# Cross-attention of a decoder layer, reordered by key blocks: maxima turned once per tile and sent as rows by DMA, pair sums on GpSimd, loop unrolled

## The chip, the cores and the metric

One core of a Trainium2 chip. The metric is the device time of one execution in microseconds (us), the median of several runs; lower is better.

## What is computed

A pre-norm decoder layer on x of shape (16, 256, 512), float32: windowed self-attention, cross-attention, a mixture-of-experts part. Each adds its output to x. The change touches only the cross-attention:

```python
def _L0_xattn_ref(q, k, v, gamma):      # q = layernorm(x); k = v = ctx
    qh = q.reshape(B, h, dq, Lq)        # B 16, h 8 heads, dq 32, Lq = Lk = 512
    kh = k.reshape(B, h, dq, Lk)
    vh = v.reshape(B, h, dv, Lk)
    qk = jnp.einsum('bhdq,bhdl->bhql', qh, kh) * scale
    sm = jax.nn.softmax(qk, axis=-1)
    ret = jnp.einsum('bhql,bhdl->bhdq', sm, vh)
    return gamma * ret.reshape(B, Dv, Lq)
```

The 256 rows of the sequence play the part of channels (8 heads of 32), and the 512 model dimensions are the positions that attend to each other.

## The kernel before

The kernel runs four stages one behind the other: `layer_norm_1`, `self_attention`, `cross_attention` and `expert_mix`. In `cross_attention` the work is cut into 32 tiles (`TILES`) of 128 partitions, each with four heads (`XPT`) of 32 rows and 512 columns; the 512 keys of a head are four blocks of 128 (`CB`).

Each tile goes through these steps. SyncE (SP) loads the tile of x and of the context. VectorE normalizes x (`normed`, L1002), ScalarE rounds it to the matmul's type (`q_round`, L946), GpSimd computes the remainders of x and of the context and also rounds the context (`split`, L803 to L807). SP writes both parts of each to DRAM (`write_parts`) and reads them back stacked, three parts of 32 rows per head, so that one matmul over 96 rows gives a product of nearly full precision (`read_stacks`, two halves of two heads, L766 and L767). TensorE computes the scores SC, queries on partitions (`scores`, L833, 16 per tile); VectorE takes the negated maxima over the keys from PSUM (`maxima`, L1008) and splits them into two parts (`max_parts`). Four groups of matmuls against the identity turn the maxima of a head into rows (`max_rows`, L842), which ScalarE copies into rows 96 to 127 of the query stack (`max_row`, L941). TensorE then computes the scores a second time, transposed, with the maxima already subtracted (`transposed_scores`, ST, L851), and ScalarE takes the exponential into `prt` (L969). Two kinds of f32 groups of four heads weigh the values (into OB) and sum the exponentials by a matmul with ones (into SU) (`output`, L864), four of each per tile. The sums are turned (`sums_by_query`, L873), inverted on VectorE (`one_over_sums`, L1022), repeated by ScalarE (`repeat`), turned back (`inverses`, L881); VectorE multiplies (`output`, L1026), adds to x (`residual`, L1030) and takes the statistics of the next norm (L1037 to L1046).

The order on each engine is written out by hand in `item`. Heads are the outer loop of a tile: the scores are two heads ahead of the transposed scores, the maximum's rows one, and the output matmuls belong to the tile before (`OUT_AT`). Scores and transposed scores have two PSUM banks each, so a score matmul waits for the maximum two before it:

```python
pe.wait_ge(s_mx, 16 * n + 4 * h + q - 1)
```

The first two and last two tiles are written out; the 28 between run in a hardware loop of 4 tiles a turn (2 on SP, `all_tiles`).

Of the kernel before, what the change touches and what calls it, by code (L numbers as in the profile page):

```python
# [625 lines left out]
def cross_attention(nc, x1, ctx_in, gamma, sq, sk, mv2, mv3, x2, cst):  # L626

    ident = cst["ident"]
    ctx = ExitStack()
    with ctx:
# [10 lines left out]
        KS = PARTS * XD  # L646
        gam = sb("gam", [P, 1], F32)
        tmp = sb("rs_tmp2", [P, 2, TILES], F32)
        rstd = sb("rstd2", [P, TILES], F32)
        cin = sb("cin", [P, 2, D], F32)  # L650
# [3 lines left out]
        qst = [sb(f"qst{i}", [P, XPT, D], F32R) for i in range(2)]  # L654
        kst = [sb(f"kst{i}", [P, XPT, D], F32R) for i in range(2)]
        vt = sb("vt", [P, 2, CB, P], F32)
        prt = [sb(f"xprt{i}", [P, XPT, CB, D], F32) for i in range(2)]
        nmx = sb("xnmx", [P, 2, CB], F32)
        nmp = sb("xnmp", [P, 2, CB, XD], F32R)
# [3 lines left out]
        osb = sb("xosb", [P, D], F32)  # L663
# [3 lines left out]
        agg = sb("agg3", [P, 2], F32)  # L667
        hold = sb("hold3", [P, 1], F32)
        SC = [pb(f"xsc{i}") for i in range(2)]
        ST = [pb(f"xst{i}") for i in range(2)]  # L670
        MB = pb("xmb")
# [5 lines left out]
        s_xi = [sem(f"x_xi{i}") for i in range(2)]  # L677
        s_ci = [sem(f"x_ci{i}") for i in range(2)]
# [3 lines left out]

        s_st = [[sem(f"x_st{i}{k}") for k in range(2)] for i in range(2)]
        s_ones = sem("x_ones")
        s_vt, s_vte = sem("x_vt"), sem("x_vte")
        s_sc = sem("x_sc")
        s_mx = sem("x_mx")
        s_nm = sem("x_nm")
        s_mr = sem("x_mr")
        s_row = sem("x_row")  # L690
        s_ts = sem("x_ts")
        s_exp = sem("x_exp")
        s_pv = sem("x_pv")
        s_oe = sem("x_oe")
        s_sq = sem("x_sq")
        s_ri = sem("x_ri")
        s_rr = sem("x_rr")
        s_rt = sem("x_rt")
        s_on = sem("x_on")
        s_x2 = sem("x_x2")  # L700
        s_bn, s_mv = sem("x_bn"), sem("x_mv")
# [5 lines left out]
        def col(ap, n):  # L707

            return ap[:, n, :] if isinstance(n, int) else ap[:, bass.ds(n, 1), :].rearrange("p o d -> p (o d)")

        def all_tiles(eng, item, unroll=4):

            item(0, 0, True, True, True)
            item(1, 1, False, True, True)

            with eng.Fori(1, 1 + (TILES - 4) // unroll) as i:
                for k in range(unroll):
                    item(unroll * i + (2 - unroll + k), k % 2, False, True, True)
            item(TILES - 2, 0, False, True, False)
            item(TILES - 1, 1, False, False, False)  # L720

        def ahead(n, h, d, more):

            return (n, h + d, True) if h + d < XPT else (n + 1, h + d - XPT, more)

        def stacks(n, t):

            per = 32 * PARTS
            return per * (n // 2 + 1) if isinstance(n, int) else (per // 2) * (n - t) + per

        def loads(n, t):

            return 16 * (n // 2 + 1) if isinstance(n, int) else 8 * (n - t) + 16

        @block.sync
        def _(sp):
            sp.dma_start(gam[:, :], gamma.rearrange("(a b) -> a b", a=1).broadcast_to([P, 1])).then_inc(s_gam, 16)

            def load(n, t, b=None):
                dst = x2[:, n, :] if isinstance(n, int) else x2[:, bass.ds(n, 1), :].rearrange("p o d -> p (o d)")  # L740
                if isinstance(n, int):
                    src, csrc = x1v[n // 2, t], cv[n]
                else:
                    src = x1v[bass.ds(b, 1), t].rearrange("o p d -> (o p) d")
                    csrc = cv[bass.ds(n, 1)].rearrange("o p d -> (o p) d")
                sp.dma_start(dst, src).then_inc(s_xi[t], 16)
                sp.dma_start(cin[:, t, :], csrc).then_inc(s_ci[t], 16)

            def write_parts(count, t):

                sp.dma_start(sq[t].rearrange("h p d -> p h d"), qp[:, :, :].bitcast(F32)).then_inc(s_qw, 16)
                sp.wait_ge(s_klo, count)
                sp.dma_start(sk[t].rearrange("h p d -> p h d"), kp[:, :, :].bitcast(F32)).then_inc(s_kw, 16)

            def parts_written(n):
                sp.wait_ge(s_qw, 16 * n + 16)
                sp.wait_ge(s_kw, 16 * n + 16)

            def read_stacks(t, k):

                hs = slice(2 * k, 2 * k + 2)
                qv = sq[t].rearrange("h (j r) d -> h r j d", j=XPT)
                kv = sk[t].rearrange("h (j r) d -> h r j d", j=XPT)
                for c in range(PARTS):
                    rows = slice(XD * c, XD * (c + 1))
                    sp.dma_start(qst[t][rows, hs, :].bitcast(F32), qv[c // 2][:, hs]).then_inc(s_st[t][k], 16)  # L766
                    sp.dma_start(kst[t][rows, hs, :].bitcast(F32), kv[c % 2][:, hs]).then_inc(s_st[t][k], 16)  # L767

            for t in range(2):
                load(t, t)  # L770
            for t in range(2):
                sp.wait_ge(s_qlo, t + 1)
                write_parts(t + 1, t)
                parts_written(t)
                for k in range(2):
                    read_stacks(t, k)

            def item(n, t, first, more, more2):
                if more2:
                    b = None if isinstance(n, int) else sp.snap((n - t) // 2 + 1)  # L780
                    sp.wait_ge(s_vt, n + 1)
                    sp.wait_ge(s_klo, n + 1)
                    load(n + 2, t, b)
                    sp.wait_ge(s_qlo, n + 3)

                    for k in range(2):
                        sp.wait_ge(s_st[t][k], stacks(n, t))
                    write_parts(n + 3, t)
                    parts_written(n + 2)
                    for k in range(2):  # L790
                        sp.wait_ge(s_ts, 16 * n + 8 * k + 8)
                        read_stacks(t, k)

            all_tiles(sp, item, 2)

        @block.gpsimd
        def _(pool):
            def split(n, t):
                pool.wait_ge(s_ci[t], loads(n, t))
                pool.wait_ge(s_kw, 16 * n)  # L800
                pool.wait_ge(s_qhi, n + 1)
                pool.wait_ge(s_qw, 16 * n)
                nc.gpsimd.tensor_tensor(qp[:, 1, :], xn[:, :], qp[:, 0, :].bitcast(F32),  # L803
                                        ALU.subtract).then_inc(s_qlo, 1)
                nc.gpsimd.tensor_copy(kp[:, 0, :], cin[:, t, :]).then_inc(s_khi, 1)
                pool.wait_ge(s_khi, n + 1)
                nc.gpsimd.tensor_tensor(kp[:, 1, :], cin[:, t, :], kp[:, 0, :].bitcast(F32),  # L807
                                        ALU.subtract).then_inc(s_klo, 1)

            for k, (dst, value) in enumerate(((kst[0][KS:P, :, :].bitcast(F32), 1.0), (ones[:, :], 1.0),  # L810
                                              (kst[1][KS:P, :, :].bitcast(F32), 1.0),
                                              (nmp[:, :, :, :].bitcast(F32), 0.0))):
                nc.gpsimd.memset(dst, value).then_inc(s_ones, 1)
                pool.wait_ge(s_ones, k + 1)
            for t in range(2):
                split(t, t)

            def item(n, t, first, more, more2):
                if more2:
                    split(n + 2, t)  # L820

            all_tiles(pool, item)

        @block.tensor
        def _(pe):
            def early(n, h, k):

                return isinstance(n, int) and 16 * n + 4 * h + k < 2

            def scores(n, t, h, q):  # L830
                if not early(n, h, q):
                    pe.wait_ge(s_mx, 16 * n + 4 * h + q - 1)
                nc.tensor.matmul(SC[q % 2][:, :], qst[t][0:KS, h, q * P:(q + 1) * P], kst[t][0:KS, h, :],  # L833
                                 start=True, stop=True).then_inc(s_sc, 1)

            def max_rows(n, t, h):

                pe.wait_ge(s_nm, 8 * n + 2 * h + 2)
                if not (isinstance(n, int) and n == 0 and h == 0):
                    pe.wait_ge(s_row, 4 * n + h)  # L840
                for q in range(CB):
                    last = nc.tensor.matmul(MB[KS:P, q * P:(q + 1) * P], nmp[:, h % 2, q, :].bitcast(F32), ident[:, :],  # L842
                                            start=True, stop=True)
                last.then_inc(s_mr, 1)
# [640 lines left out]
```

## Time and profile before

| | us |
|---|---|
| median of 3 runs | 3128.82 (3126.6 to 3129.32) |
| profiled execution, its own time | 3131.23 |
| its span | 3129.5 |
| TensorE matmul busy in the span | 2908.0 (93%) |
| VectorE busy | 1889.7 (60%) |
| ScalarE busy | 1082.9 (35%) |
| GpSimd busy | 607.1 (19%) |

Cross-attention runs from about 2025 to 2830 us of the span. The profile is of one execution. PE is TensorE's matmul, PEld its weight load, DVE VectorE, ACT ScalarE, POOL GpSimd, SP SyncE, which issues DMAs. "Granted clock" is TensorE's clock as a share of 2.4 GHz. In a timeline a row is start, length, engine, line, operation, output<-inputs, count; a bracket is the idle time before it and what ended it. A DVE or POOL row begins when the engine has begun the instruction, whether or not it can proceed.

### The profile page before, as it was taken

The numbers are of one execution on the slowest core, as the hardware profiler recorded it, in microseconds if no ns is written. First come the engines' busy times: TensorE is split into PE (matmuls) and PEld (weight loads), VectorE is DVE, ScalarE is ACT, GpSimd is POOL, SyncE is SP. The second block draws the span as 40 slices with busy tenths as digits, with TensorE's granted clock in tenths as the row PEclk, the third lists the DMA queues.
The fourth block names the chain that finished last, engine by engine and source line by source line (L and its number), as shares of the span: only waits on it lengthen the run. The fifth ranks groups of instructions, "written<-read, shape, count | busy, mean of one in ns | idle before, by whom it ended". The sixth has DMA issues, their size and how long they took to land. (4 is left out here: it accounts for less than half of the span.)

```text
span 3129.5 us, 45670 instructions
## 1 busy us (share of the span) xinstructions
PE 2908.0 (93%) x15230; PEld 2163.0 (69%) x15230; DVE 1889.7 (60%) x3899; ACT 1082.9 (35%) x2575; POOL 607.1 (19%) x530
## 2 busy tenths in 40 slices
PE   3799999999999999999999999799999999997974
PEld 2588888888888888888788888544544445447852
DVE  7465565665665665565566666565656656553488
ACT  2222223222223222223222222255555555553321
POOL 2111112221112221112321111111111111100163
PEclk9999999999999999999999999989999999995597
DMA  8411222231122131132232121164444444420002
GB/s 315 155 61 54 81 82 85 79 107 54 60 103 81 68 121 54 55 108 78 71 106 70 54 83 53 69 173 130 123 122 132 134 134 121 128 68 17 0 0 107
DMA packets 166225, 289.33 MB, mean 92 GB/s; under 512 B 13728, under 2 KB 79264, under 8 KB 164000
## 3 DMA queue, kind: packets, MB, share of 16 engines
q1 hardware_dynamic: 166048, 287.14, 28.5%
q8 instruction: 90, 1.47, 0.2%
q14 instruction: 87, 0.71, 0.1%
HBM read 194.81 MB, written 92.27 MB: 92 GB/s over the span
## 5 line engine op out<-in xcount | busy, mean ns | idle before, releaser
L439 PE MATMUL pj<-xnt,whi 128*128 128x512 f32 x2048 | 706.8, 407 | 16.1 <-DMA xnt<-xt_scratch 16.1
L519 ACT ACTIVATE pr<-sc,nmx 128x128 f32<-128x128 f32 (+1 forms) x512 | 211.1, 417 | 936.4 <-DVE nmx L591 936.4
L1008 DVE TENSOR_REDUCE xnmx<-xsc 128x1 f32<-128x512 f32 x512 | 340.0, 688 | 277.6 <-PE xsc L833 241.9
L439 PEld LDWEIGHTS pj<-xnt,whi 128*128 128x128 f32 x2048 | 387.4, 189 | 109.1 <-DMA xnt<-xt_scratch 16.5
L969 ACT ACTIVATE xprt<-xst 128x512 f32<-128x512 f32 x512 | 298.4, 596 | 308.1 <-PE xst L851 305.5
L439 PE MATMUL pj<-xnt,wlo 128*128 128x512 f32 x1024 | 400.2, 391 | 0.0
L394 POOL TENSOR_TENSOR qt<-rot,swp 128x512 f32<-128x512 f32 x128 | 166.1, 1297 | 1129.3 <-DVE swp L572 1129.3
L436 PE MATMUL pj<-whi,xnt 128*128 128x512 f32 x1024 | 351.7, 405 | 0.0
L570 DVE TENSOR_TENSOR rot<-pj,trig 128x512 f32<-128x512 f32 x256 | 177.0, 691 | 230.2 <-PE pj L439 230.2
L833 PE MATMUL xsc<-kst,qst 96*128 96x512 f32 x512 | 248.7, 487 | 46.9 <-DVE xnmx L1008 24.2
L833 PEld LDWEIGHTS xsc<-kst,qst 96*128 96x128 f32 x512 | 99.5, 195 | 275.3 <-DVE xnmx L1008 158.7
L591 DVE TENSOR_REDUCE nmx<-sc 128x1 f32<-128x128 f32 (+1 forms) x512 | 158.6, 352 | 177.5 <-PE sc L465 173.0
L600 DVE TENSOR_SCALAR pr<-pr,rinv 128x128 f32<-128x128 f32 (+1 forms) x512 | 251.4, 532 | 9.0
L436 PEld LDWEIGHTS pj<-whi,xnt 128*128 128x128 f32 x1024 | 192.4, 188 | 45.9
L394 POOL TENSOR_TENSOR kt<-rot,swp 128x512 f32<-128x512 f32 x128 | 165.3, 1292 | 297.5 <-DVE swp L572 297.5
L439 PEld LDWEIGHTS pj<-xnt,wlo 128*128 128x128 f32 x1024 | 194.8, 190 | 34.9
L452 PE MATMUL pj<-whi,ohi 128*128 128x512 f32 x512 | 212.5, 415 | 1.4 <-DVE olo L605 1.4
L851 PE MATMUL xst<-qst,kst 128*128 128x512 f32 x512 | 212.1, 415 | 1.3 <-ACT qst L941 1.3
L579 DVE TENSOR_TENSOR xio<-pj,xio 128x512 f32<-128x512 f32 x128 | 88.5, 692 | 192.2 <-PE pj L452 192.2
L452 PE MATMUL pj<-whi,olo 128*128 128x512 f32 x512 | 201.6, 394 | 0.0
L436 PE MATMUL pj<-wlo,xnt 128*128 128x512 f32 x512 | 199.1, 389 | 0.0
L452 PE MATMUL pj<-wlo,ohi 128*128 128x512 f32 x512 | 199.1, 389 | 0.0
(159 smaller groups left out, 4885.6 us busy)
## 6 DMA issues: line engine op xcount, KB each, us to landing
xnt<-xt_scratch SPq DMA_DIRECT2D x64, 1024.0 KB, 8.0
x_scratch<-xio SPq DMA_DIRECT2D x64, 512.0 KB, 3.6
xio<-x_scratch SPq DMA_DIRECT2D x48, 512.0 KB, 4.1
qst<-sq_scratch SPq DMA_DIRECT2D x192, 128.0 KB, 3.0
kst<-sk_scratch SPq DMA_DIRECT2D x192, 128.0 KB, 3.2
xt_scratch<-parts SPq DMA_DIRECT2D x16, 1024.0 KB, 4.7
sq_scratch<-qp SPq DMA_DIRECT2D x32, 512.0 KB, 2.8
sk_scratch<-kp SPq DMA_DIRECT2D x32, 512.0 KB, 2.8
```

The lines of the kernel that those rows point to most:

```text
L394: nc.gpsimd.tensor_tensor(qk["QK".index(kind)][h][:, :, :].rearrange("p b n -> p (b n)"), rot[r % 2][:, :], swp[r % 2][:, :], ALU.add).the ...
L436: last = nc.tensor.matmul(bank[:, :], moving[:, i * P:(i + 1) * P], wpart[:, w, :], start=(k == 0), stop=(k == 3 * CB - 1))
L439: last = nc.tensor.matmul(bank[:, :], wpart[:, w, i * HD:(i + 1) * HD], moving, start=(k == 0), stop=(k == 3 * CB - 1))
L452: last = nc.tensor.matmul(PJ[n % 3][:, :], o[:, h, tok], w[:, CH_O + h, :], start=(h == 0 and k == 0), stop=(h == HG - 1 and k == 2))
L519: nc.scalar.activation(pr[:, a % 4, lo:hi], SC[a % 2][:, lo:hi], ACT.Exp, bias=nmx[:, a % 4, t:t + 1], accum_out=rsum[:, a % 4, t:t + 1]). ...
L570: nc.vector.tensor_tensor(ro, bank, table(slice(0, P), q), ALU.mult)
L591: nc.vector.tensor_reduce(nmx[:, a % 4, t:t + 1], SC[a % 2][:, lo:hi], AX.X, ALU.max, negate=True).then_inc(s_nmx, 1)
L600: nc.vector.tensor_scalar(pr[:, a % 4, lo:hi], pr[:, a % 4, lo:hi], rinv[:, a % 4, t:t + 1], None, ALU.mult).then_inc(s_pr, 1)
L833: nc.tensor.matmul(SC[q % 2][:, :], qst[t][0:KS, h, q * P:(q + 1) * P], kst[t][0:KS, h, :], start=True, stop=True).then_inc(s_sc, 1)
L851: nc.tensor.matmul(ST[c % 2][:, :], kst[t][:, h, c * P:(c + 1) * P], qst[t][:, h, :], start=True, stop=True).then_inc(s_ts, 1)
L969: nc.scalar.activation(prt[t][:, h, c, :], ST[c % 2][:, :], ACT.Exp).then_inc(s_exp, 1)
L1008: nc.vector.tensor_reduce(nmx[:, h % 2, q:q + 1], SC[q % 2][:, :], AX.X, ALU.max, negate=True).then_inc(s_mx, 1)
```

## The change

The head loop and the key-block loop of a tile change places. A step s is one key block c of a tile n (s = 4n + c), with the four heads inside. In a step TensorE issues, for i = 0 to 3, a score matmul of step s+6 (`AHEAD`, a head of the tile one and a half ahead) and the transposed score of head i, after i = 1 some other work (`middle`), and last the output group of step s-1. All loops are unrolled in Python.

The 16 columns of maxima of a tile are turned by one transpose into MX, rounded by ScalarE and their remainder taken by VectorE, and two DMAs place them as rows 96 and 97 of the query stack; the key stack has ones there. The exponentials lie in a ring of five buffers, one per step. GpSimd adds those of two steps in place (`pair_sum`, 128x2048), and TensorE's sums with ones run on the pairs, two groups a tile. The context is rounded by ScalarE. Stacks are three deep, loads four, and each stack is read by six DMAs in place of twelve. The memsets that held scheduling apart and the copy of the statistics go.

```diff
         PARTS = 3
         KS = PARTS * XD
+        KM = KS + 2
+        AHEAD = 6
+        RING = 5
+        STACKS = 3
...
@@ sync @@
+            def read_stacks(m):
+                sp.wait_ge(s_qw, 16 * m + 16)
+                sp.wait_ge(s_kw, 16 * m + 16)
+                if m >= STACKS:
+                    sp.wait_ge(s_ts, 16 * (m - STACKS) + 16)
...
+            def max_rows(m):
+                for k, (part, here) in enumerate(((mhi, s_mhi), (mlo, s_mlo))):
+                    sp.wait_ge(here, m + 1)
+                    row = qst[m % STACKS][KS + k:KS + k + 1, :, :].rearrange("o h (q n) -> o (h q) n", n=P)
+                    sp.dma_start(row.bitcast(F32), part[:, :].bitcast(F32)).then_inc(s_row[m % STACKS], 16)
+
+            for n in range(-4, TILES):
+                if tile(n + 2):
+                    read_stacks(n + 2)
+                if tile(n + 1):
+                    max_rows(n + 1)
+                if tile(n + 3):
+                    write_parts(n + 3)
+                if tile(n + 4):
+                    load(n + 4)
@@ gpsimd @@
+            def pair_sum(n, k):
+                s = CB * n + 2 * k
+                a, b = prt[s % RING], prt[(s + 1) % RING]
+                pool.wait_ge(s_exp, 4 * (s + 1) + 4)
+                pool.wait_ge(s_pv, s + 1)
+                nc.gpsimd.tensor_tensor(a[:, :, :].rearrange("p h n -> p (h n)"), a[:, :, :].rearrange("p h n -> p (h n)"),
+                                        b[:, :, :].rearrange("p h n -> p (h n)"), ALU.add).then_inc(s_add, 1)
...
+            for n in range(-3, TILES + 1):
+                if tile(n - 1):
+                    pair_sum(n - 1, 1)
+                if tile(n + 3):
+                    split(n + 3)
+                if tile(n):
+                    pair_sum(n, 0)
@@ tensor @@
+            def scores(g, q):
+                m, h = g // CB, g % CB
+                if h == 0 and q == 0:
+                    pe.wait_ge(s_st[m % STACKS], 16 * 2 * PARTS * (m // STACKS + 1))
+                if 4 * g + q >= 2:
+                    pe.wait_ge(s_mx, 4 * g + q - 1)
...
+            def transposed_scores(s, h):
+                n, c = s // CB, s % CB
+                if c == 0 and h == 0:
+                    pe.wait_ge(s_row[n % STACKS], 32 * (n // STACKS + 1))
+                if 4 * s + h >= 2:
+                    pe.wait_ge(s_exp, 4 * s + h - 1)
...
+            def sums(n, k):
+                pe.wait_ge(s_add, 2 * n + k + 1)
...
+            def max_transposes(n):
+                pe.wait_ge(s_mx, 16 * n + 16)
+                pe.wait_ge(s_mlo, n)
+                nc.tensor.transpose(MX[0:XPT * CB, 0:P], nmx[:, n % 2, :], ident[:, :]).then_inc(s_mt, 1)
...
+            def middle(n, c):
+                if c == 0:
+                    if tile(n - 1):
+                        sums(n - 1, 0)
+                    if tile(n):
+                        values(n)
+                if c == 1 and tile(n - 2):
+                    inverses(n - 2)
+                if c == 2:
+                    if tile(n - 1):
+                        sums(n - 1, 1)
+                    if tile(n + 1):
+                        max_transposes(n + 1)
+                if c == 3 and tile(n - 1):
+                    sums_by_query(n - 1)
+
+            for s in range(FIRST, LAST):
+                for i in range(XPT):
+                    if 0 <= s + AHEAD < STEPS:
+                        scores(s + AHEAD, i)
+                    if 0 <= s < STEPS:
+                        transposed_scores(s, i)
+                    if i == 1:
+                        middle(s // CB, s % CB)
+                if 0 <= s - 1 < STEPS:
+                    weigh(s - 1)
@@ scalar, keys are (key block, head) @@
+            WORK = {(0, 1): ((repeat, -2),), (0, 2): ((v_evac, 0),), (1, 0): ((output_evac, -1),), (1, 1): ((q_round, 3),),
+                    (1, 2): ((k_round, 3),), (2, 2): ((max_round, 1),), (2, 3): ((sums_evac, -1),)}
@@ vector @@
+            def max_rest(n):
+                dve.wait_ge(s_mhi, n + 1)
+                nc.vector.tensor_tensor(mlo[:, :], MX[0:XPT * CB, 0:P], mhi[:, :].bitcast(F32),
+                                        ALU.subtract).then_inc(s_mlo, 1)
...
+            WORK = {(0, 0): ((normed, 3),), (2, 0): ((output, -2),), (2, 1): ((residual, -2),), (2, 2): ((max_rest, 1),),
+                    (3, 0): ((statistics, -2),), (3, 1): ((mean_and_variance, -2),), (3, 3): ((one_over_sums, -1),)}
+
+            for s in range(FIRST, LAST):
+                n, c = s // CB, s % CB
+                for q in range(XPT):
+                    if 0 <= s + AHEAD < STEPS:
+                        maximum(s + AHEAD, q)
+                    for do, d in WORK.get((c, q), ()):
+                        if tile(n + d):
+                            do(n + d)
```

## Rows read from the trace of the kernel before

**Rows 1.** Busy time by windows: us, busy PE PEld DVE ACT POOL (count), PEclk, DMA, GB/s

```profile
2047.60:2790.60 743.00, 718.58 (x4377) 367.28 (x4376) 452.69 (x1007) 434.18 (x769) 93.53 (x90) 0.97 0.46 129
2132.40:2155.10 22.70, 22.70 (x145) 11.62 (x144) 14.75 (x34) 14.10 (x25) 3.12 (x3) 1.00 0.46 132
2177.80:2208.90 31.10, 27.39 (x146) 14.11 (x145) 14.97 (x35) 14.10 (x25) 3.12 (x3) 0.84 0.36 102
...
1524.50:1527.70 3.20, 3.20 (x9) 2.52 (x8) 2.50 (x6) 0.20 (x1) 1.28 (x1) 0.50 0.87 328
```

**Rows 2.** Groups by line, page of the profile: busy us, mean ns, idle before

```profile
L969 ACT ACTIVATE xprt<-xst 128x512 f32<-128x512 f32 x512 | 298.4, 596 | 308.1 <-PE xst L851 305.5
...
L1030 DVE SCALAR_TENSOR_TENSOR x<-xonm,gam,x 128x512 f32 x28 | 21.1, 752 | 0.0
```

**Rows 3.** Timeline of one tile, 2405 to 2412 us: start, us, engine, line

```profile
2405.49 0.50 PE L833 MATMUL xsc<-kst,qst 96*128 96x512 f32 x1
...
2405.83 0.40 PE L851 MATMUL xst<-qst,kst 128*128 128x512 f32 x1
...
2406.03 0.69 DVE L1008 TENSOR_REDUCE xnmx<-xsc 128x1 f32<-128x512 f32 x1
2406.07 0.60 PE L911 MATMUL xvb<-ident,cin 128*128 128x128 f32 x4
...
2406.42 0.48 PE L833 MATMUL xsc<-kst,qst 96*128 96x512 f32 x1
...
2408.63 0.40 PE L833 MATMUL xsc<-kst,qst 96*128 96x512 f32 x1
...
2408.86 0.39 PE L851 MATMUL xst<-qst,kst 128*128 128x512 f32 x1
...
2409.18 1.06 PE L864 MATMUL xob<-xprt,vt 128*32 128x512 f32 x8
...
2410.18 0.50 PE L833 MATMUL xsc<-kst,qst 96*128 96x512 f32 x1
...
2410.74 0.95 PE L873 MATMUL xvb<-ident,xssb 128*128 128x4 f32 x8
...
2411.55 0.48 PE L833 MATMUL xsc<-kst,qst 96*128 96x512 f32 x1
```

**Rows 4.** Timeline of the first layer norm, 24 to 26 us: VectorE beside GpSimd

```profile
24.15 1.27 POOL L155 TENSOR_TENSOR wlo<-wraw,whi 128x512 fp32r<-128x512 f32 x1 [2.53 <-ACT whi L212]
...
24.90 0.81 DVE L166 TENSOR_SCALAR xn<-x_all,mv,rstd 128x512 f32<-128x512 f32 x1
```

**Rows 5.** Timeline of the threshold search, 2979 us on: VectorE beside GpSimd

```profile
2979.61 1.29 POOL L1296 TENSOR_TENSOR z<-z,eb 128x512 f32 x1
...
2979.72 1.22 DVE L1375 TENSOR_TENSOR thr<-thr,add 128x16 int32<-128x16 int32 x1
...
2980.97 0.18 DVE L1377 TENSOR_TENSOR cand<-thr,bits 128x16 int32<-128x16 int32 x1
```

**Rows 6.** Durations of GpSimd lines, ns min/median/max

```profile
L1286 POOL TENSOR_TENSOR held_out<-hold x32: 194/194/647, 2954.2 to 3085.4; 128x1 f32<-128x1 f32 x32
L803 POOL TENSOR_TENSOR qp<-xn,qp x32: 1262/1282/1288, 2026.6 to 2757.0; 128x512 fp32r<-128x512 f32 x32
L805 POOL CAST kp<-cin x32: 604/611/617, 2027.8 to 2758.2; 128x512 fp32r<-128x512 f32 x32
```

**Rows 7.** Timeline of TensorE at 1523 us, idle time in brackets

```profile
1522.99 0.67 PE L484 MATMUL ob<-prt,v 128*128 128x256 f32 x2 [2.21 <-DVE olo L605]
```

**Rows 8.** DMA view, 2400 to 2448 us: GB/s in 40 slices

```profile
GB/s 237 5 253 232 219 253 200 224 328 36 0 0 0 0 0 0 85 352 237 200 36 234 234 220 253 193 210 302 73 0 0 0 0 0 0 14 384 251 225 17
```

**Rows 9.** Timeline at both ends of the cross-attention

```profile
2038.25 1.19 PE L833 MATMUL xsc<-kst,qst 96*128 96x512 f32 x2 [22.54 <-DMA kst<-sk_scratch]
...
2829.87 0.17 DVE L1046 COPY mv<-agg 128x2 f32<-128x2 f32 x1
```

More of the change, by code:

```diff
@@ L662, in cross_attention @@
         rrep = sb("xrrep", [P, CB, P], F32)
-        osb = sb("xosb", [P, D], F32)
+        osb = [sb(f"xosb{i}", [P, D], F32) for i in range(2)]
         ssb = sb("xssb", [P, D], F32)
@@ L676, in cross_attention @@
         s_gam, s_var, s_sqrt, s_step = sem("x_gam"), sem("x_var"), sem("x_sqrt"), sem("x_step")
[L677 to L678 removed]
+        s_xi = [sem(f"x_xi{i}") for i in range(4)]
+        s_ci = [sem(f"x_ci{i}") for i in range(4)]
         s_qn, s_qhi, s_qlo = sem("x_qn"), sem("x_qhi"), sem("x_qlo")
@@ L705, in cross_attention, with tile @@
         x1v = x1.rearrange("b p t d -> b t p d")
[L707 to L733, printed above, removed]
+        FIRST, LAST = -4 * CB, CB * (TILES + 2)
+        def tile(n):
+            return 0 <= n < TILES
         @block.sync
@@ L778, in item @@
[L778 to L792, printed above, removed]
@@ L824, in _ @@
+            for i in range(STACKS):
+                nc.gpsimd.memset(kst[i][KS:KM, :, :].bitcast(F32), 1.0).then_inc(s_ones, 1)
+                pool.wait_ge(s_ones, i + 1)
+            nc.gpsimd.memset(ones[:, :], 1.0).then_inc(s_ones, 1)
+            for n in range(-3, TILES + 1):
[5 more added lines that the diff above has]
+                    pair_sum(n, 0)
         @block.tensor
@@ L825, in _ @@
         def _(pe):
[L826 to L844, printed above, removed]
@@ L846, in transposed_scores @@
-            def transposed_scores(n, t, h, c):
-                if c == 0:
-                    pe.wait_ge(s_row, 4 * n + h + 1)
-                if not early(n, h, c):
-                    pe.wait_ge(s_exp, 16 * n + 4 * h + c - 1)
-                nc.tensor.matmul(ST[c % 2][:, :], kst[t][:, h, c * P:(c + 1) * P], qst[t][:, h, :],
-                                 start=True, stop=True).then_inc(s_ts, 1)
-            def output(n, t, c, banks=(0, 1)):
-                if c == 0 and 0 in banks:
-                    pe.wait_ge(s_exp, 16 * n + 16)
-                    pe.wait_ge(s_vte, n + 1)
-                    pe.wait_ge(s_oe, 2 * n)
-                for k in banks:
-                    for h in range(XPT):
-                        rows = slice(XD * h, XD * (h + 1))
-                        last = nc.tensor.matmul((OB, SU)[k][rows, :], (vt[:, t, c, rows], ones[:, :])[k],
-                                                prt[t][:, h, c, :], start=(c == 0), stop=(c == CB - 1))
-                if c == CB - 1 and 1 in banks:
-                    last.then_inc(s_pv, 1)
+            def scores(g, q):
[4 more added lines that the diff above has]
+                    pe.wait_ge(s_mx, 4 * g + q - 1)
+                nc.tensor.matmul(SC[q % 2][:, :], qst[m % STACKS][0:KS, h, q * P:(q + 1) * P],
+                                 kst[m % STACKS][0:KS, h, :], start=True, stop=True).then_inc(s_sc, 1)
@@ new lines, in transposed_scores, with weigh @@
+            def transposed_scores(s, h):
[4 more added lines that the diff above has]
+                    pe.wait_ge(s_exp, 4 * s + h - 1)
+                nc.tensor.matmul(ST[h % 2][:, :], kst[n % STACKS][0:KM, h, c * P:(c + 1) * P],
+                                 qst[n % STACKS][0:KM, h, :], start=True, stop=True).then_inc(s_ts, 1)
+            def weigh(s):
+                n, c = s // CB, s % CB
+                pe.wait_ge(s_exp, 4 * s + 4)
+                pe.wait_ge(s_vte, n + 1)
+                if c == 0:
+                    pe.wait_ge(s_oe, n)
+                for h in range(XPT):
+                    rows = slice(XD * h, XD * (h + 1))
+                    last = nc.tensor.matmul(OB[rows, :], vt[:, n % 2, c, rows], prt[s % RING][:, h, :],
+                                            start=(c == 0), stop=(c == CB - 1))
+                last.then_inc(s_pv, 1)
@@ new lines, in sums, with values @@
+            def sums(n, k):
+                pe.wait_ge(s_add, 2 * n + k + 1)
+                if k == 0:
+                    pe.wait_ge(s_se, n)
+                for h in range(XPT):
+                    rows = slice(XD * h, XD * (h + 1))
+                    last = nc.tensor.matmul(SU[rows, :], ones[:, :], prt[(CB * n + 2 * k) % RING][:, h, :],
+                                            start=(k == 0), stop=(k == 1))
+                last.then_inc(s_su, 1)
+            def values(n):
+                pe.wait_ge(s_ci[n % 4], 16 * (n // 4 + 1))
+                if n >= 2:
+                    pe.wait_ge(s_ri, n - 1)
+                for c in range(CB):
+                    last = nc.tensor.transpose(VB[:, c * P:(c + 1) * P], cin[:, n % 4, c * P:(c + 1) * P], ident[:, :])
+                last.then_inc(s_vt, 1)
@@ L926, in _ @@
-            all_tiles(pe, item)
-            for c in range(CB):
-                output(TILES - 1, 1, c)
-            for n in (TILES - 2, TILES - 1):
-                pe.wait_ge(s_vte, TILES)
-                pe.wait_ge(s_x2, n + 1)
-                sums_by_query(n)
-                inverses(n)
+            def middle(n, c):
[13 more added lines that the diff above has]
+                    sums_by_query(n - 1)
@@ L995, in _ @@
             dve.wait_ge(s_gam, 16)
-            nc.vector.memset(hold[:, :], 0.0).then_inc(s_x2, 1)
-            def normed(n, t):
-                dve.wait_ge(s_xi[t], loads(n, t))
-                dve.wait_ge(s_qlo, n)
-                i = slice(n, n + 1) if isinstance(n, int) else bass.ds(n, 1)
-                nc.vector.tensor_scalar(xn[:, :], col(x2, n), mv2[:, i, 0], rstd[:, i],
-                                        ALU.subtract, ALU.mult).then_inc(s_qn, 1)
-            def maxima(n, h, banks):
-                for q in banks:
-                    dve.wait_ge(s_sc, 16 * n + 4 * h + q + 1)
-                    nc.vector.tensor_reduce(nmx[:, h % 2, q:q + 1], SC[q % 2][:, :], AX.X, ALU.max,
-                                            negate=True).then_inc(s_mx, 1)
@@ L1011, in max_parts, with normed @@
-            def max_parts(n, h):
-                dve.wait_ge(s_mx, 16 * n + 4 * h + 4)
-                if not (isinstance(n, int) and n == 0 and h < 2):
-                    dve.wait_ge(s_mr, 4 * n + h - 1)
-                nc.vector.tensor_copy(nmp[:, h % 2, :, 0], nmx[:, h % 2, :]).then_inc(s_nm, 1)
-                dve.wait_ge(s_nm, 8 * n + 2 * h + 1)
-                nc.vector.tensor_tensor(nmp[:, h % 2, :, 1], nmx[:, h % 2, :], nmp[:, h % 2, :, 0].bitcast(F32),
-                                        ALU.subtract).then_inc(s_nm, 1)
+            def normed(m):
+                dve.wait_ge(s_xi[m % 4], 16 * (m // 4 + 1))
+                dve.wait_ge(s_qlo, m)
+                nc.vector.tensor_scalar(xn[:, :], x2[:, m, :], mv2[:, m, 0:1], rstd[:, m:m + 1],
+                                        ALU.subtract, ALU.mult).then_inc(s_qn, 1)
@@ L1042, in mean_and_variance @@
-                nc.vector.bn_aggr(agg[:, :], bn[:, :]).then_inc(s_bn, 1)
-            def keep_statistics(n):
-                dve.wait_ge(s_bn, 2 * n + 2)
-                nc.vector.tensor_copy(col(mv3, n), agg[:, :]).then_inc(s_mv, 1)
-            def between(n, t, h, k, first, more2):
-                work = {(1, 0): (one_over_sums,), (2, 0): (output,), (2, 1): (residual,), (3, 0): (statistics,),
-                        (3, 1): (mean_and_variance, keep_statistics)}
-                second = isinstance(n, int) and n == 1
-                if not first and not second:
-                    for do in work.get((h, k), ()):
-                        do(n - 2)
-                if more2 and (h, k) == (1, 1):
-                    normed(n + 2, t)
@@ L1059, in _ @@
-            for t in range(2):
-                normed(t, t)
-            dve.wait_ge(s_ones, 4)
-            for h in range(2):
-                maxima(0, h, range(CB))
-                max_parts(0, h)
-            def item(n, t, first, more, more2):
-                for h in range(XPT):
-                    n2, h2, there2 = ahead(n, h, 2, more)
-                    for k in range(2):
-                        if there2:
-                            maxima(n2, h2, (2 * k, 2 * k + 1))
-                        if k == 1 and there2:
-                            max_parts(n2, h2)
-                        between(n, t, h, k, first, more2)
@@ L1076, in _ @@
-            all_tiles(dve, item)
-            for n in (TILES - 2, TILES - 1):
-                one_over_sums(n)
-                for finish in (output, residual, statistics, mean_and_variance, keep_statistics):
-                    finish(n)
-            dve.wait_ge(s_mv, TILES)
+                nc.vector.bn_aggr(mv3[:, n, :], bn[:, :]).then_inc(s_bn, 1)
+            WORK = {(0, 0): ((normed, 3),), (2, 0): ((output, -2),), (2, 1): ((residual, -2),), (2, 2): ((max_rest, 1),),
+                    (3, 0): ((statistics, -2),), (3, 1): ((mean_and_variance, -2),), (3, 3): ((one_over_sums, -1),)}
@@ L1084, in expert_mix @@
+            for s in range(FIRST, LAST):
+                n, c = s // CB, s % CB
+                for q in range(XPT):
+                    if 0 <= s + AHEAD < STEPS:
+                        maximum(s + AHEAD, q)
+                    for do, d in WORK.get((c, q), ()):
+                        if tile(n + d):
+                            do(n + d)
+            dve.wait_ge(s_bn, 2 * TILES)
 def expert_mix(nc, router_w, router_b, expert_w, expert_b, mv3, x2, out, cst):
```

256 lines of the change are left out of this document (97 added, 159 removed).

## The prediction, made before the changed kernel was timed

> **What bounds the kernel now.** I read the busy shares in slices first: from 2025 to 2830 us, the cross-attention, TensorE is full, while VectorE and ScalarE stand near six tenths. The table by windows says the same of one tile of 128 queries [rows 1]: in 22.7 us TensorE is busy for 22.7, VectorE for 14.75, ScalarE for 14.1, GpSimd for 3.1. The mean tile is longer, (2790.61 - 2047.56) / 31 = 23.97 us between the first and last transposes of the values, because six of the 31 tiles, one at each turn of the hardware loop, take 28 to 32 us. In the one shown TensorE stands still for 3.7 us and its granted clock falls (0.84 on average) [rows 1]. The six cost 44 us over the common length. So TensorE's list of work sets the end, and an edit is worth what it takes from that list, until another engine or a wait becomes the limit.
>
> **TensorE's list after the change.** The starts in the timeline give the price of each item [rows 3]. A score matmul (SC) to the next transposed score (TS) is 0.34 us behind a foreign group and 0.23 otherwise; TS to a foreign group is 0.32. Eight f32 passes of one group take 0.99 to the next SC (9.18 to 10.18), and a second group in the same gap 0.86 more. Four transposes of values take 0.35, the sums by query 0.81. The change removes the four groups that make rows of the maxima and two of the four that sum by ones, since pairs are added beforehand: six f32 groups per tile, 6 x 0.86 = 5.2 us, and some gaps between kinds. A step (one key block, four SC, four TS) is SC, TS, SC, TS, the middle, the same four again, then one output group: 3.25 us plus the middle. The middles are 1.22 + 0.1 (sums and values), 0.35 (inverses), 0.87 + 0.2 (sums and one transpose of maxima) and 0.72 (sums by query). Together 4.55 + 3.6 + 4.35 + 4.0 = 16.5 us a tile against 22.75. Unrolling also removes the loop's turns. If nothing else bound, that would be over 200 us.
>
> **The other engines.** VectorE keeps 16 maxima of 0.69 us [rows 3] and about 3.3 us of small work: 14.3 of 16.5. ScalarE keeps 16 exponentials of 0.60 [rows 2], loses four row copies and gains one rounding: 13.5. Both would fit. The PSUM banks stay two deep, so a pause of VectorE of more than about 1.4 us stops TensorE: SC number k waits for maximum k-2. GpSimd gets two sums of 128x2048 per tile. No row has that size. Between one column (0.194 us) and 512 columns (1.282) [rows 6] the slope is 2.13 ns a column, so 2048 cost 0.19 + 4.36 = 4.5 us; four times the 512 row, 5.1, is the upper bound, and 2.4, the one-input rate of the cast (0.611 for 512), the lower, which two inputs have not reached. I take 4.5, since both ends of that line are of the same operation. With the two splits GpSimd has 11.6 us a tile, which fits too. The Trainium skill, GPSIMD Engine Reference, section on reconciling with measured numbers, has 4497 ns for this sum.
>
> **What long GpSimd instructions do to VectorE.** Here the trace speaks against the change. A `tensor_scalar` from SBUF to SBUF that takes 0.54 us elsewhere took 0.81 when it began inside a GpSimd subtract: that ended at 25.42, VectorE at 25.71 [rows 4]. A 16-column `tensor_tensor` with two SBUF inputs took 1.22 us beside GpSimd's add, and its like, just behind it, 0.18 [rows 5]. VectorE waited for the end of GpSimd's instruction in both. The maxima, read from PSUM, show no such lengths: 0.69 [rows 3] is also their mean. The Trainium skill, SBUF — State Buffer, section on the two sides, has this as an exclusive lock held for the full instruction. The rows here show it for 1.3 us instructions; I carry it over to 4.5. Two VectorE instructions per tile have these forms: `normed` (SBUF to SBUF) and `residual` (two SBUF inputs; alone 0.75 [rows 2]).
>
> *First stall.* `pair_sum(n-1, 1)` waits for the output group issued last in step 4n-1 and so starts 0.1 us after step 4n begins (I set time 0 there) and ends at 4.6. `normed` stands behind maximum 0, which starts 0.54 after its SC [rows 3] and ends at 1.23. It is inside the sum, by 1.1 us of margin, and ends at 4.9. Maxima 1, 2, 3 are queued behind it; maximum 1 ends at 5.55, and SC 3, due at 3.0, waits for it: 2.6 us lost. Step 4n+1 begins at 7.2 instead of 4.55.
>
> *Second stall.* ScalarE in step 4n+1 does exp, output copy, exp, q rounding, which ends 3.2 us into the step; the two splits follow (1.28 each), so `pair_sum(n, 0)` starts about 5.8 into it, or 1.9 us into step 4n+2. `residual` comes behind maximum, product, maximum: 2.35 into step 4n+2. GpSimd is first by 0.45 us, close, and `residual` waits to 6.4, ends at 7.0; maximum 2 ends at 7.6. The next step's first SC needs it and starts 3.3 us late. Step 4n+3 pays another 0.3 for `max_rest`. Sum: 7.2 + 3.9 + 7.6 + 4.3 = 23.0 us a tile.
>
> *Clock.* TensorE then idles for 2.4 and 3.2 us in every tile. In the trace an idle of 2.21 us [rows 7] was followed by a stretch at a granted clock of 0.50, 1.2 GHz [rows 1]; so was the idle of 3.7 us at the loop's turn, in a tile at 0.84. There TensorE's items take up to twice as long. A short such stretch after each stall costs about 1.7 us in step 4n+3, 0.5 to 1 in the rest of step 4n and step 4n+1 (part hides in the next stall). I take 2.5, which gives 25.5 us; the ends are 23.0 (clock holds) and 28 (it stays low over half the tile; then items at 1.2 GHz cover the first stall).
>
> **DMA and rows.** Bytes per tile stay at 3.07 MB, at some 230 to 250 GB/s while transfers run [rows 8]: 12.5 us, in any tile length above hidden. SP now waits for the maxima's rows before it writes the next parts, and the stack reads follow the writes. From the end of `max_rest` that chain is 0.9 (issues) + 5.3 (writes) + 8.5 (loads ahead, 1.57 MB of reads) = 14.7 us to the scores. With the second stall the cycle is 8.0 + 14.7 = 22.7, just under 23.0; without stalls 4.1 + 14.7 = 18.8, so it and not TensorE's 16.5 would be the floor. The row itself lands some 3 us after its copy and is needed 4 later. The added rounding on ScalarE replaces GpSimd's cast; unrolled code costs nothing as long as instructions arrive, as they did inside the loop body.
>
> **Ends.** Before, the first scores start at 2038.25 and the last copy is at 2829.87 [rows 9]. After, the stack of a whole tile must land (+3 us), and 24 scores at 0.8 us run before the first exponential: first TS near 2061. The last three tiles lose their `normed` and then their scores: 18.5 + 15 + 14.5. The tail is 14 us (one 4.5 us sum in it). Tiles 0 and 1 have no `residual`: 19.5 each. With T for the 27 others the stage ends at 2061 + 39 + 48 + 14 + 27 T = 2162 + 27 T. T = 25.5 gives 2850.5 against 2830: 20 us later. The profiled execution took 3131.2 us (span 3129.5), 2.4 above the median of 3128.8, so 3151 there is 3149 in the median. Break-even is T = 24.7.
>
> **Rivals.**
> 1. *Both stalls, clock mostly holds*, T near 23.0: 2162 + 621 = 2783, 47 us faster, 3082. For it: the clock shown in [rows 1] also recovers within the tile. Against: an idle of 2.2 us already lowered it. 0.17.
> 2. *Only the first stall*: `residual` gets in ahead of the sum, decided by those 0.45 us. T = 7.2 + 3.6 + 4.4 + 4.0 = 19.2, with some lost clock 20.2; the end is 2123 + 29 x 20.2 = 2709, and the time 3007. 0.18.
> 3. *No stall*: long sums do not hold VectorE. T = the DMA chain's 18.7, end 2665, time about 2960. The rows on short instructions speak against it. 0.09.
> 4. *Clock low for more than half of each tile*, T = 28: end 2918, 3215. For it: a mean of 0.84 over the 31 us of [rows 1] means 10 us at half clock behind one idle. 0.08.
>
> The forecast, both stalls and short slow stretches, has 0.48; its own range is T = 24.3 to 27, 3115 to 3190. Most of it is slower, 0.40; 0.05 within 0.2% (6 us, about what a measurement of this kernel can tell), 0.03 faster. With the rivals: faster 0.03 + 0.17 + 0.18 + 0.09 = 0.47, same 0.05, slower 0.48. The range from 2990 to 3205 leaves out rival 3, rival 4 and little else.
>
> **What would show it.** `normed` and `residual` lasting about 4 us each in VectorE's rows, with TensorE's SC waiting on the maxima twice per tile; sums of 4.5 us on GpSimd; granted clock below 0.9 over the stage; row DMAs that no TS waits for. If `residual` keeps 0.75 us, rival 2 holds; if both keep their lengths, rival 3. If TensorE waits for stack DMAs instead, my DMA chain was short.

## The result, and the profile after

The changed kernel takes 3169.4 us in the median (3163.2 to 3170.2) against 3129.1 (3126.6 to 3129.5): a ratio of 1.0126, 95% interval 1.0109 to 1.0144. It is slower by 40 us; 20 were forecast.

The table by windows, over the 26 tiles between the third and the twenty-ninth, and behind one of TensorE's stalls (columns as in [rows 1]):

```profile
2106.50:2783.40 676.90, 548.88 (x2527) 267.13 (x2523) 511.15 (x599) 315.18 (x599) 301.38 (x105) 0.83 0.48 123
2408.80:2416.00 7.20, 7.20 (x25) 4.03 (x25) 4.15 (x9) 2.39 (x4) 0.00 (x0) 0.53 0.72 240
```

A tile takes 676.9 / 26 = 26.0 us (24.7 to 27.3), against a mean of 23.97 before. TensorE is busy for 81% of it where it had been busy for all of a common tile [rows 1], and its granted clock is 0.83. VectorE's busy time rose from 14.75 to 19.7 us a tile, though it has less to do. The groups by line say where that is (durations in ns: min/median/max; one from each line's own view):

```profile
L954 DVE TENSOR_SCALAR xn<-x,mv,rstd x32: 537/3640/4235, 2025.7 to 2782.4; 128x512 f32<-128x512 f32 x32
```
```profile
L982 DVE SCALAR_TENSOR_TENSOR x<-xonm,gam,x x32: 752/4308/4362, 2117.9 to 2868.6; 128x512 f32<-128x512 f32 x32
```
```profile
L763 POOL TENSOR_TENSOR xprt<-xprt x64: 4522/4552/4932, 2074.6 to 2857.5; 128x2048 f32<-128x2048 f32 x64
```

`normed` (L954) has 3.64 us in the median where it had 0.55, `residual` (L982) 4.31 where it had 0.75 [rows 2]. The pair sum takes 4.55 us. The timeline around both stalls of one tile:

```profile
2403.04 4.55 POOL L763 TENSOR_TENSOR xprt<-xprt 128x2048 f32<-128x2048 f32 x1
...
2403.78 4.36 DVE L982 SCALAR_TENSOR_TENSOR x<-xonm,gam,x 128x512 f32<-128x512 f32 x1
...
2408.79 0.56 PE L786 MATMUL xsc<-kst,qst 96*128 96x512 f32 x1 [2.99 <-DVE xnmx L963]
...
2416.25 4.56 POOL L763 TENSOR_TENSOR xprt<-xprt 128x2048 f32<-128x2048 f32 x1 [8.67 <-PE xob L806]
...
2417.14 3.95 DVE L954 TENSOR_SCALAR xn<-x,mv,rstd 128x512 f32<-128x512 f32 x1
...
2421.75 0.50 PE L786 MATMUL xsc<-kst,qst 96*128 96x512 f32 x1 [2.48 <-DVE xnmx L963]
```

The sum ends at 2407.59 and `residual` at 2408.14; the next sum ends at 2420.81 and `normed` at 2421.09. Both begin inside a sum and end 0.3 to 0.55 us behind it. Then the maxima queued behind them run, and TensorE, idle for 2.99 and 2.48 us, goes on. The granted clock, 1.00 from 2404.50 to 2408.80, is 0.53 in the 7.2 us behind the first of these idle times (2408.80 to 2416.00, in the table above) and 0.79 in the 8.2 us behind the second. The view of waits of the stage names the same cause (us in total, times, longest; its rows of ScalarE and GpSimd are left out, since these engines have time):

```profile
PEld xsc L786 <- DVE xnmx L963: 219.0, 141, 3.9
...
PE xsc L786 <- DVE xnmx L963: 137.3, 57, 3.0
...
PEld xsc L786 <- DMA kst<-sk_scratch: 4.6, 3, 2.9
```

TensorE itself stood still for a maximum 57 times, for 2.4 us in the mean: about twice a tile. It hardly waits for the stacks here (4.6 us in all for its weight loads), and no transposed score waits for a DMA of rows.

### The profile page after: what moved, and what is told of

Same layout as the page of the kernel before. It is cut to its first block and busy times, and to the rows that moved or that the text cites. A ratio compares the mean times of both kernels' runs of the same rounds, so it can differ in the third digit from the quotient of the medians.

```text
span 3168.2 us, 39780 instructions
## 1 busy us (share of the span) xinstructions
PE 2826.1 (89%) x13725; PEld 2101.8 (66%) x13726; DVE 2017.4 (64%) x3578; ACT 1018.9 (32%) x2511; POOL 880.0 (28%) x562
## 5 line engine op out<-in xcount | busy, mean ns | idle before, releaser
L786 PE MATMUL xsc<-kst,qst 96*128 96x512 f32 x512 | 279.5, 550 | 169.3 <-DVE xnmx L963 139.1
L763 POOL TENSOR_TENSOR xprt<-xprt 128x2048 f32<-128x2048 f32 x64 | 291.7, 4558 | 256.9 <-PE xob L806 256.9
L786 PEld LDWEIGHTS xsc<-kst,qst 96*128 96x128 f32 x512 | 118.6, 232 | 353.2 <-DVE xnmx L963 228.5
L795 PE MATMUL xst<-qst,kst 98*128 98x512 f32 x512 | 238.4, 469 | 0.8 <-ACT xprt L900 0.5
```

The costliest lines, as they stand in the source:

```text
L763: nc.gpsimd.tensor_tensor(a[:, :, :].rearrange("p h n -> p (h n)"), a[:, :, :].rearrange("p h n -> p (h n)"), b[:, :, :].rearrange("p h n ...
L786: nc.tensor.matmul(SC[q % 2][:, :], qst[m % STACKS][0:KS, h, q * P:(q + 1) * P], kst[m % STACKS][0:KS, h, :], start=True, stop=True).then_ ...
L795: nc.tensor.matmul(ST[h % 2][:, :], kst[n % STACKS][0:KM, h, c * P:(c + 1) * P], qst[n % STACKS][0:KM, h, :], start=True, stop=True).then_ ...
```

## The experiments

Each is timed against the kernel before; the times are medians of four runs (five for rows_last). They come from three sessions, in which the kernel before took 3130.5, 3131.5 and 3128.3 us; each ratio is to the one of its own session. Line numbers of the changed kernel differ from those before.

**1. Only `normed` moved.** GpSimd is idle in the first half of step 4n+1.

```diff
-            WORK = {(0, 0): ((normed, 3),), ...
+            WORK = {(1, 0): ((normed, 3),), ...
```

> VectorE's normed goes from behind maximum (0, 0) to behind (1, 0), where GpSimd is idle. Lock theory (VectorE waits for the end of a GpSimd instruction when it reads or writes SBUF through the shared side): normed drops from 3.6 us to 0.55, the first stall of a tile (2.5 us) goes with part of the slow clock behind it, residual still takes 4.3 us; tile from 26.1 to about 22.5, time about 3169 - 29 x 3.6 = 3065. Rival (the order by key blocks or the rows by DMA costs the time, and the long rows of normed are only an effect): under 20 us of change.

Measured: 3041.6 us, 0.9721 of before (0.9704 to 0.9737). `normed` is back at 0.54, and the maxima behind it come in time:

```profile
L954 DVE TENSOR_SCALAR xn<-x,mv,rstd x32: 535/537/1840, 2021.9 to 2664.7; 128x512 f32<-128x512 f32 x32
```

One entry of a table gives 128 us, where the lock theory had expected 104. That is more than one stall: `residual` fell from 4.31 to 1.50 us in the median as well. It still ends 0.55 us behind the sum, but begins some 3.5 us into it, since TensorE now waits for its stacks at the start of that step, and the maxima in front of `residual` come later.

**2. Only `residual` moved**, with its statistics a tile later and a wait that keeps its input.

```diff
-            WORK = {..., (2, 1): ((residual, -2),), (3, 0): ((statistics, -2),), ...
+            WORK = {..., (1, 0): ((residual, -3),), (3, 0): ((statistics, -3),), ...
```

> VectorE's residual goes from behind (2, 1) to the next tile's (1, 0), statistics with it one tile later; normed stays where it is. Lock theory: residual drops from 4.3 us to 0.75, the second stall (2.9 us) goes, normed still takes 3.6 us; tile about 22, time about 3050. Rival (order or rows cost it): under 20 us of change.

Measured: 3038.8 us, 0.9713 (0.9696 to 0.9731). The expectation was about 3050. `residual` is at its own 0.74 in all 32 tiles, `normed` still at 2.66 (it begins later than in the change, behind the load of its x, and is held to the sum's end). A tile takes 21.2 us. The waits between 2200 and 2600 us show what is left:

```profile
PE xsc L786 <- DVE xnmx L963: 50.3, 26, 2.8
PEld xsc L786 <- DMA kst<-sk_scratch: 3.6, 4, 1.1
```

TensorE waits for the maxima behind `normed`, the first stall, and hardly for the stacks; its granted clock there is 0.91.

**3. Both moved.**

```diff
...
+            WORK = {(0, 0): ((statistics, -3),), (0, 1): ((mean_and_variance, -3),), (1, 0): ((normed, 3),), (2, 0): ((output, -2),),
+                    (2, 2): ((max_rest, 1),), (3, 2): ((residual, -2),), (3, 3): ((one_over_sums, -1),)}
```

> normed behind (1, 0), residual behind (3, 2), statistics in the next tile; GpSimd's sums as before. Lock theory: both at their own lengths, no stall of over 1 us on VectorE's side, clock 1.0; then either TensorE's list (16.5 us a tile) or the chain rows, parts written, stacks read (18.7) bounds it: tile 18.7 to 19.5, time 2955 to 2985. Rival (the sums themselves are late for TensorE or the ring): TensorE waits for GpSimd's sums, tile over 22.

Measured: 3038.4 us, 0.9708 (0.9692 to 0.9724). Nothing is held any longer (0.54 and 0.74 us in the median), and yet it is no faster than either move alone. The expectation for the two operations held, the one for the time did not. The waits between 2200 and 2600 us name a new one:

```profile
PE xsc L786 <- DMA kst<-sk_scratch: 45.1, 18, 3.9
```

TensorE waits for the stacks, 18 times in 19 tiles. In experiment 1 the same row has 45.2 us, also 18 times: the DMA chain is the bound of that run too, but not of experiment 2. The sync queue shows why:

```profile
2302.79 1.26 POOL L755 TENSOR_TENSOR kp<-cin,kp 128x512 fp32r<-128x512 f32 x1
...
2309.98 0.28 DVE L968 TENSOR_TENSOR xmlo<-xmx,xmhi 16x128 fp32r<-16x128 f32 x1 [0.51 <-ACT xmhi L924]
2310.53 0.59 SPq L736 DMA_DIRECT2D qst<-xmlo  x1
2311.16 0.58 SPq L716 DMA_DIRECT2D sq_scratch<-qp  x1
...
2315.98 0.32 SPq L729 DMA_DIRECT2D qst<-sq_scratch  x1
```
```profile
2325.56 0.50 PE L786 MATMUL xsc<-kst,qst 96*128 96x512 f32 x1 [1.97 <-DMA kst<-sk_scratch]
```

The parts are ready at 2304.05 but are written at 2311.16, behind the row of maxima; the reads follow, and TensorE gets its stack at 2325.56. From the end of `max_rest` (2310.26) that is 15.3 us, where the prediction had 14.7; and `max_rest` ended 5.2 us into its step, not 4.1. The cycle is 20.5 us in this tile, not 18.8, and 21.3 in the mean, at a granted clock of 0.90. That the slow clock makes up the difference is not shown.

Not every VectorE instruction is held beside a sum. In this run the statistics (SBUF to SBUF, one input) began at 2295.12, inside a sum that ran from 2294.23 to 2298.81, and took 0.68 us; none of the 32 took over 0.70. The product of `output`, with one input in SBUF and one in PSUM, took 0.68 inside a sum in experiment 1 (2306.11, sum from 2304.16 to 2308.71).

**4. SyncE's order changed, on top of 3.**

```diff
-                if tile(n + 1):
-                    max_rows(n + 1)
                 if tile(n + 3):
                     write_parts(n + 3)
+                if tile(n + 1):
+                    max_rows(n + 1)
```

> both_moved with SyncE's order changed: the parts of tile n+3 are written to DRAM before SyncE waits for the maxima of tile n+1. In both_moved the parts were ready some 7 us before they were written (2304 against 2311 us), since SyncE stood at the wait for the rows; TensorE then waited 3.3 us a tile for the stacks. Chain theory: writes 7 us earlier, no wait on stacks, no slow clock; TensorE's list is the bound, tile 16.5 to 17.5, time 2900 to 2925. Rival (bandwidth: 3.07 MB a tile is what takes the time): tile stays over 20, time 3030.

Measured: 2921.9 us, 0.9332 (0.9319 to 0.9345): 210 us faster than before, 248 faster than the change. TensorE from 2200 to 2600 us:

```profile
2200.00:2600.00 400.00, 388.61 (x2263) 187.48 (x2255) 300.61 (x526) 272.84 (x536) 267.39 (x89) 1.00 0.65 170
```

It is busy for 97%, at full clock, a tile takes 17.2 us, and the bytes of a tile, unchanged, move at 170 GB/s, against 150 in experiment 3 over the same window and 123 in the change. So bandwidth was not what held experiment 3. The order of one queue was.

**5. The same order alone, in the changed kernel.**

> The changed kernel with SyncE's order alone changed: parts written before the wait for the rows; normed and residual stay where they are held. Theory: the DMA chain (22.7 us) lay under the two stalls (26.1 us a tile), TensorE hardly ever waited for stacks, so nothing comes back: within 15 us of 3169. Rival (the chain was itself a cost of the change): 3130 or less.

Measured: 3165.5 us, 1.0114 (1.0097 to 1.013); the clock over the same 26 tiles is 0.83 again, and TensorE is idle for as long. The DMA chain lay wholly under the two stalls. The same edit is worth 4 us there, no more than the runs of one kernel differ by, and 117 in experiment 4.

**6. The sums taken from GpSimd.** GpSimd's pair sums go; TensorE sums each step behind its output group; the copy of the sums moves to step 4n+1.

```diff
...
                 if 0 <= s - 1 < STEPS:
                     weigh(s - 1)
+                    sums((s - 1) // CB, (s - 1) % CB)
```

> No sums on GpSimd: TensorE sums every step with ones behind its output group, four groups a tile in place of two, all else as in the changed kernel. Lock theory: normed 0.55 and residual 0.75 to 2 us (a 1.28 us split may still hold it); TensorE's list 18.0 us, the DMA chain 18.7; tile 18.7 to 19.5, time 2955 to 2985, faster than both kernels although TensorE has 1.7 us more work a tile. Rival (TensorE's work is what counts and the pair sums save it): slower than the changed kernel by 1.7 x 32 = 55 us, 3225.

Measured: 3007.3 us, 0.9612 (0.9596 to 0.9628), 22 us above the expected range. With `normed` and `residual` where the change put them, both keep their own lengths, 0.54 and 0.74 in the median:

```profile
L970 DVE SCALAR_TENSOR_TENSOR x<-xonm,gam,x x32: 740/743/753, 2112.4 to 2702.6; 128x512 f32<-128x512 f32 x32
```

Giving TensorE the work back makes the kernel 162 us faster: the sums on GpSimd are what held VectorE. The tile is 20.0 us, above the 18.7 expected; the next run shows that the stacks are not the reason.

**7. Experiment 6 with SyncE's new order.**

> sums_on_tensor with SyncE's order changed too; against rows_last it shows what GpSimd's pair sums are worth once nothing holds VectorE. TensorE's list is 18.0 us against 16.5, so tile 18.2 to 19 against 17.2, time 2950 to 2975: 1.2 to 1.6 us x 32 slower than rows_last's 2922. If ScalarE's or VectorE's share were the bound in both, no difference.

Measured: 3003.7 us, 0.9599 (0.9583 to 0.9615): a miss, 29 us above the range. The tile stays at 20.0 us and the time falls by only 4, so the DMA chain was not the bound. In the 20 tiles from 2200 to 2600 us TensorE is busy for 375.8 us, 18.8 a tile where 18.0 were expected, and waits 1.2 us a tile for PSUM banks: 14.0 us in 40 waits for a maximum and 10.3 in 20 for an exponential. That this comes from the two groups in a row at the end of a step, which crowd the scores into the rest, is a guess that no run tests. Against experiment 4 GpSimd's sums are worth 82 us, 2.6 a tile; there TensorE is busy for 16.7 us a tile, 2.1 less. (`normed` and `residual` are also at different places in the two, which was not separated.)

**8. The sums in four instructions each**, nothing moved.

```diff
-                nc.gpsimd.tensor_tensor(a[:, :, :].rearrange("p h n -> p (h n)"), a[:, :, :].rearrange("p h n -> p (h n)"),
-                                        b[:, :, :].rearrange("p h n -> p (h n)"), ALU.add).then_inc(s_add, 1)
+                for h in range(XPT):
+                    last = nc.gpsimd.tensor_tensor(a[:, h, :], a[:, h, :], b[:, h, :], ALU.add)
+                last.then_inc(s_add, 1)
```

> The changed kernel with each pair sum as four GpSimd instructions of 128x512 in place of one of 128x2048; nothing moved. If VectorE waits for the one GpSimd instruction that runs, normed and residual wait 1.3 us at most: median under 2 us for each in place of 3.6 and 4.3, both stalls below 1 us, and the DMA chain bounds as in both_moved: 3035 to 3060. If VectorE waits until GpSimd has no sum left (four in a row, 5.1 us), no change or up to 30 us slower than 3169.

Measured: 3025.3 us, 0.9665 (0.9649 to 0.9682), 10 us below the expected range.

```profile
L955 DVE TENSOR_SCALAR xn<-x,mv,rstd x32: 536/823/1839, 2022.7 to 2641.5; 128x512 f32<-128x512 f32 x32
```
```profile
2308.56 5.17 POOL L764 TENSOR_TENSOR xprt<-xprt 128x512 f32<-128x512 f32 x4 [6.74 <-PE xob L807]
...
2309.91 1.45 DVE L955 TENSOR_SCALAR xn<-x,mv,rstd 128x512 f32<-128x512 f32 x1 [0.37 <-DMA x<-x_scratch]
```

`residual` has 1.33 us in the median and 1.89 at most, so the longest wait is now that of one short instruction (1.28 us) with VectorE's own part. In the timeline `normed` ends at 2311.36, 0.2 us behind the end of the second of four sums in a row and 2.4 before the end of the last: VectorE is let in between two GpSimd instructions that stand back to back. So it waits for the instruction that runs, not for an idle GpSimd. The four together are longer than one, and the kernel is still 144 us faster than the change.

**9. Useless matmuls where TensorE stalls.**

```diff
+            def filler(count):
+                for _ in range(count):
+                    nc.tensor.matmul(MX[KS:P, P:2 * P], ident[:, KS:P], ident[:, :], start=True, stop=True)
...
+                if s % CB == 3 and 0 <= s - 8 < STEPS - 8:
+                    filler(13)
...
+                    if s % CB == 0 and i == 3 and 0 <= s < STEPS - 12:
+                        filler(10)
```

> The changed kernel with useless matmuls (128x32 by 128x128, f32, into unused rows of the maxima's bank) where TensorE stalls: 10 behind the third pair of step 4n, 13 ahead of step 4n+3, about 2.1 and 2.8 us at 2.4 GHz. Clock theory (of the 26.1 us a tile, 3 are the slow clock that the idle brings): clock up to above 0.97, tile 23 to 24, time 3169 - 29 x 2.5 = 3095, with 4.9 us more work a tile. Rival (the lengths come from VectorE alone): 3169 or slower.

Measured: 3091.2 us, 0.9874 (0.9859 to 0.9889), 78 us faster than the change with 4.9 us more work in most tiles:

```profile
2106.50:2783.40 676.90, 657.97 (x4198) 376.43 (x4197) 522.00 (x662) 353.74 (x681) 340.86 (x114) 1.00 0.49 128
```

Granted clock 1.00 in place of 0.83, and nearly every tile at 22.8 to 22.9 us. This is the tile with both stalls and no lost clock, for which the prediction had 23.0. The other 3.1 us of the 26.0 are the clock. `residual` still takes 4.35 us in the median, and `normed` still ends 0.29 us behind the sum that it began in: VectorE is held as before. (`normed` itself has 2.81 us in the median, since it begins later, behind the load of its x.)

**10. The kernel before, unrolled.**

```diff
-            with eng.Fori(1, 1 + (TILES - 4) // unroll) as i:
-                for k in range(unroll):
-                    item(unroll * i + (2 - unroll + k), k % 2, False, True, True)
+            for n in range(2, TILES - 2):
+                item(n, n % 2, False, True, True)
```

> The kernel before with its hardware loops over the tiles written out, nothing else. The six long tiles (28 to 32 us) become 22.75: 44 us less, 3085. If long tiles come at the same places without a loop, the cause was not the loop: 3129.

Measured: 3086.5 us, 0.9856 (0.9841 to 0.9871): 45 us against 44 expected. From the third tile on, all are 22.75 to 22.8 us. The turns of the loop cost what the six long tiles had shown [rows 1]. The Trainium skill, Runtime: NRT & Kernel Launch, section on instruction fetch, says that a taken branch can make a sequencer fetch its target before it goes on; the run agrees in that the gaps go with the branch, and does not show the fetch itself. So the change took 45 us from unrolling alone and lost 85 elsewhere.

## Why the prediction was right, point by point

- **TensorE's list**: 16.5 us forecast. In experiment 4 a tile takes 17.2, of which TensorE is busy for 16.7; the rest are short waits on banks and on stacks.
- **Length of a sum**: 4.5 from the line through [rows 6], 4.55 measured. The trace agrees with the Trainium skill, GPSIMD Engine Reference, section on elementwise work side by side, which has 4497 ns for this instruction.
- **VectorE waits for GpSimd's instruction**: carried over from 1.3 us instructions [rows 4, 5] to 4.5. Shown by experiments 1, 2, 6 and 8, each of which takes the coincidence or its length away; experiment 3 has forms that are not held. It is also what the Trainium skill, SBUF — State Buffer, section on the two sides, calls a lock for the full instruction; experiment 8 agrees with "instruction" as the unit.
- **First stall**: `normed` began 0.9 us behind the sum's start in the tile shown and 1.2 in most (1.1 forecast), TensorE idle 2.48 (2.4 forecast).
- **Second stall**: `residual` 0.74 behind the sum's start (0.45 forecast), TensorE idle 2.99 (3.2 forecast). The race I had called close went the forecast way in the first 28 of the 32 tiles; of the last four one `residual` was held (2.18 us).
- **Clock**: 2.5 us a tile taken, 3.1 measured (26.0 less experiment 9's 22.9). Right in kind, too small.
- **Ends**: the first transposed score came at 2063.8 for 2061, and the stage ended at 2870.3 for 2850.5. Of the 20 us missing, 27 x 0.5 = 14 are the tile (mostly the clock), 3 the start and 3 the rest.
- **The DMA chain** as a floor below the stalls: right, and hidden, as experiments 3 to 5 show. Its size was wrong: 20.5 us for 18.8. That makes one rival too cheap: *no stall*, 2960, measures 3038 (experiment 3).
- **Rival 2, only the first stall**: 3007 forecast; it measures 3039 (experiment 2), and not for that floor: TensorE waited 3.6 us in 400 for stacks there. Of its tile of 21.2 us, 16.7 are TensorE's work at full clock (experiment 4) and 2.7 its idle time, which leaves some 1.8 for the slow clock, an estimate, where the rival had 1.0. So the clock was put too cheap here as well.

The sign hung on terms near each other: 45 us from the loop and over 100 from TensorE's list against two stalls and the clock. The forecast was near an even bet, and the result is in the case that had 0.48. The stalls came as worked out; the size, 40 us where 20 were forecast, was short by the clock and the two ends.

## What to carry to other kernels

Before work goes to GpSimd, list VectorE's instructions of the forms that were held here (a `scalar_tensor_tensor` with two SBUF inputs, a `tensor_scalar` from SBUF to SBUF), and place them where GpSimd is idle, or cut GpSimd's work into short instructions; what counts is the length of one GpSimd instruction, not its share. A stall of TensorE costs twice, once as idle time and once by the clock after it. And when removing a wait brings nothing, look at which queue stands at another wait with ready work behind it: here one swap in SyncE's order was worth 117 us, but only once the stalls above it were gone.

## What the runs showed of the hardware that was not expected

- Added work can shorten a kernel: 23 matmuls a tile, 4.9 us, brought the clock from 0.83 to 1.00 and took 78 us away (experiment 9).
- A loop's turn costs 5 to 10 us once in four tiles, of which about 4 are idle and the rest slow clock; straight code of 32 tiles had no such gap (experiment 10).
- Two moves worth 128 and 131 us alone are worth 131 together. With the first or with both TensorE waits 45 us in 400 for its stacks; with the second alone it does not, and the first stall and its slow clock happen to cost as much.
- VectorE's statistics and its product with one PSUM input ran at their own 0.68 us inside GpSimd's sums, while two other forms were held to the sum's end (experiments 1 and 3).
